# A new order for the first stage of a perceiver layer: context groups, the scaling of x and the weights

## The reference: what is computed

```
x = x + cross_attention(layernorm(x), ctx, w_q, w_k, w_v, w_o)   # 16 heads of 64, 4096 keys
x = x + self_attention(layernorm(x), ...)                        # heads mixed before and after a causal softmax, 16 memory keys
x = x + ffn(layernorm(x), ...)                                   # gated, 16-bit activations, 4-bit weights in blocks of 32

def layernorm(x):  return (x - mean(x)) / sqrt(var(x) + 1e-5)
def cross_attention(query, ctx, ...):
    q, k, v = query @ w_q, ctx @ w_k, ctx @ w_v                  # split into 16 heads
    return concat_heads(softmax(q @ k.T * 64 ** -0.5) @ v) @ w_o
```

## Time and profile before

| | us |
|---|---|
| median of three executions | 1400.45 (1395.76 to 1401.65) |
| the profiled execution | 1400.91 |
| its span on the core | 1398.7 |
| PE busy | 1257.7 (90%) |
| DVE, ACT, POOL busy | 879.3, 723.3, 411.8 |

### The profile page before, as it was taken

One profiled execution on the slowest core, in us unless ns is written; L12 is line 12 of the kernel. 1 busy time (PEld: TensorE's weight loads), 2 busy tenths in 40 slices (PEclk: granted clock), 3 DMA queues, 4 the chain that ended last, 5 costly groups with the idle time before them and its releaser, 6 DMA issues. The chain is left out here.

```text
span 1398.7 us, 21065 instructions
## 1 busy us (share of the span) xinstructions
PE 1257.7 (90%) x8379; PEld 939.1 (67%) x8379; DVE 879.3 (63%) x1042; ACT 723.3 (52%) x1304; POOL 411.8 (29%) x372
## 2 busy tenths in 40 slices
PE   3999999999999999899999999999999697969533
PEld 2786877777786868587868687777778443636312
DVE  5647676766766676547676767676776456513576
ACT  3655556565656556546565655655565231523152
POOL 3605051433425150414342505152342102211010
PEclk9999999999999999999999999999999798979776
DMA  4303020302021133210311203030202354250000
GB/s 154 76 1 74 7 80 1 80 1 80 18 63 50 28 78 93 74 36 2 79 42 39 60 22 79 1 80 1 76 3 63 129 95 55 35 57 1 23 0 15
DMA packets 42528, 68.19 MB, mean 49 GB/s; under 512 B 5040, under 2 KB 31152, under 8 KB 42432
## 3 DMA queue, kind: packets, MB, share of 16 engines
q1 hardware_dynamic: 40896, 66.21, 19.3%
q10 hardware_dynamic: 1536, 0.66, 0.4%
HBM read 25.89 MB, written 0.52 MB: 19 GB/s over the span
## 5 line engine op out<-in xcount | busy, mean ns | idle before, releaser
L455 DVE TENSOR_REDUCE step_max<-score_banks 128x2 f32<-128x1024 f32 x256 | 300.5, 1221 | 122.2 <-PE score_banks L579 122.2
L476 DVE TENSOR_TENSOR prob_sum<-prob_sum,probs 128x1024 f32<-128x1024 f32 x224 | 279.4, 1288 | 139.5 <-ACT probs L406 138.8
L338 POOL TENSOR_TENSOR k_split<-probs,k_split 64x512 fp32r<-64x512 f32 x128 | 163.6, 1278 | 327.6 <-ACT probs L389 323.7
L406 ACT ACTIVATE probs<-score_banks 128x1024 f32<-128x1024 f32 x181 | 181.9, 1028 | 149.4 <-PE out_ps L605 85.3
L593 PE MATMUL score_banks<-q_twice,k_split 128*128 128x256 f32 x724 | 182.2, 288 | 0.2 <-ACT probs L406 0.2
L594 PE MATMUL score_banks<-q_low_max,k_ones 128*128 128x256 f32 x724 | 178.1, 283 | 0.0
L340 POOL TENSOR_TENSOR k_split<-probs,k_split 64x512 fp32r<-64x512 f32 x128 | 163.9, 1281 | 9.6
L593 PEld LDWEIGHTS score_banks<-q_twice,k_split 128*128 128x128 f32 x724 | 138.3, 191 | 11.9 <-issue 6.2
L594 PEld LDWEIGHTS score_banks<-q_low_max,k_ones 128*128 128x128 f32 x724 | 138.5, 191 | 0.0
L331 POOL TENSOR_TENSOR w_lo<-w_raw,w_hi 128x768 fp32r<-128x768 f32 x16 | 36.2, 2260 | 336.5 <-ACT w_hi L357 336.5
L381 ACT ACTIVATE k_split<-key_banks 64x512 fp32r<-64x512 f32 x128 | 75.5, 590 | 104.7 <-PE key_banks L542 104.1
(11 more groups left out here) (207 smaller groups left out, 2169.2 us busy)
## 6 DMA issues: line engine op xcount, KB each, us to landing
k_ones<-k_split SPq DMA_DIRECT2D x128, 256.0 KB, 4.0
ctx_rows<-in_ctx_dram SPq DMA_DIRECT2D x10, 512.0 KB, 3.8
grouped_far<-dots_far SPq DMA_DIRECT2D x32, 136.0 KB
w_raw<-in_L_xattn_w_v_dram SPq DMA_DIRECT2D x14, 256.0 KB, 3.5
probs<-in_ctx_dram SPq DMA_DIRECT2D x6, 512.0 KB, 5.9
w_raw<-in_L_xattn_w_q_dram SPq DMA_DIRECT2D x16, 128.0 KB, 3.5
w_raw<-in_L_xattn_w_k_dram SPq DMA_DIRECT2D x16, 128.0 KB, 3.8
wo_pair<-in_L_xattn_w_o_dram SPq DMA_DIRECT2D x16, 128.0 KB, 2.1
```

The lines of the kernel that those rows point to most:

```text
L338: pool.tensor_tensor(k_split[DH:P, A, keys], keys_staged[j % 2][0:DH], k_split[0:DH, A, keys].bitcast(F32), ALU.subtract).then_inc(k_low[A ...
L406: act.activation(probs[:, j % 2, h, :], scores_of, ACT.Exp, scale=SCALE).then_inc(exp_done, 1)
L455: dve.tensor_reduce(step_max[:, qt, :, j], score_banks[:, 2 * qt:2 * qt + 2, :], X, ALU.max).then_inc(max_done, 1)
L476: dve.tensor_tensor(prob_sum[:, h, :], prob_sum[:, h, :], probs[:, j % 2, h, :], ALU.add).then_inc(sum_done, 1)
```

## The change

The diff reorders the first stage. On DVE, `normalise_rows` gets a callback between the statistics and the scaling, and there the low parts of groups 0, 1 and 2 are made; the copies of `xnT` come behind group 4. On POOL the clearing of the second half of `k_ones` and its row of ones move behind `w_lo` of the first pair. On ACT the row of ones moves into the key loop of the first pair, behind piece 3, and the weights of the first pair are split behind group 2. On SP the weights of the first pair are loaded behind group 0. On PE the first pass transposes groups 0 to 5, with x behind group 4; in the first pair the order is key piece 0, group 6, key piece 1, group 7, and then q. PE, ACT and POOL no longer wait for the constants at the places where they did; SP still does, before it copies into `k_ones`.

```diff
-def normalise_rows(dve, x, out, stats, moments, chain, inverse_std):
+def normalise_rows(dve, x, out, stats, moments, chain, inverse_std, between=None):
...
         dve.bn_aggr(moments[:, t, :], stats[:, t, :]).then_inc(chain, 1)
     n += TOK_TILES
+    if between is not None:
+        between()
     dve.wait_ge(inverse_std, 3)
...
                     sp.dma_start(rows_of(n), ctx_tiles[b, :, tiles, :]).then_inc(ctx_loaded[slot], 16)
-                    if n == SLOTS - 1:
+                    if n == 0:
                         load_weights(0)
...
             pool.wait_ge(inverse_std, 3)
-            pool.memset(k_ones[0:DH, B, :].bitcast(F32), 0.0).then_inc(consts_ready, 1)
-            pool.wait_ge(consts_ready, 4)
-            pool.memset(k_ones[0:1, B, :].bitcast(F32), 1.0).then_inc(consts_ready, 1)
+
+            def zeros_and_ones():
+                pool.memset(k_ones[0:DH, B, :].bitcast(F32), 0.0).then_inc(consts_ready, 1)
+                pool.wait_ge(consts_ready, 4)
+                pool.memset(k_ones[0:1, B, :].bitcast(F32), 1.0).then_inc(consts_ready, 1)
+                pool.wait_ge(consts_ready, 5)
...
                 pool.wait_ge(w_low, it + 1)
+                if it == 0:
+                    zeros_and_ones()
...
-            pool.wait_ge(consts_ready, 5)
             for b in range(BATCH):
                 pairs_of_batch(b, body)
...
-            act.wait_ge(consts_ready, 3)
-            act.activation(k_ones[DH:DH + 1, A, :], ones[DH:DH + 1, 0:1].to_broadcast([1, CTX]), ACT.Copy
-                           ).then_inc(ones_a, 1)
+            def row_of_ones():
+                act.wait_ge(consts_ready, 3)
+                act.activation(k_ones[DH:DH + 1, A, :], ones[DH:DH + 1, 0:1].to_broadcast([1, CTX]), ACT.Copy
+                               ).then_inc(ones_a, 1)
...
                     if j < STEPS and values_behind(i, j) is not None:
                         copy_v(b, i, parity, values_behind(i, j))
+                    if it == 0 and j == 3:
+                        row_of_ones()
...
                         context_high(act, n)
-                        if n == LOADS - 3:
+                        if n == 2:
                             split_weights(0, 0, 0)
-                    act.wait_ge(consts_ready, 5)
...
+            def first_contexts():
+                for n in range(3):
+                    context_low(dve, n)
+
             dve.wait_ge(x_loaded, 16)
-            normalise_rows(dve, x_res, xn, stats, moments, norm_chain, inverse_std)
+            normalise_rows(dve, x_res, xn, stats, moments, norm_chain, inverse_std, first_contexts)
...
-                for n in range(LOADS if b == 0 else 0):
+                for n in range(3, LOADS if b == 0 else 0):
                     context_low(dve, n)
-                    if n == 3:
+                    if n == 4:
                         for c in range(DC):
                             dve.wait_ge(xT_made, c + 1)
...
-                project_q(it, b)
+                if it > 0:
+                    project_q(it, b)
                 pe.wait_ge(w_low, it + 1)
                 wait_past(pe, exp_done, 2 * STEPS * it - 1)
                 for j in range(2):
                     if i == 0:
                         pe.wait_ge(ctx_low, DC * (j + 1 if b == 0 else (b + 1) * LOADS))
                     project_k(it, j)
+                    if it == 0:
+                        transpose_context(6 + j)
+                if it == 0:
+                    project_q(it, b)
...
-                for n in range(LOADS if b == 0 else 0):
+                for n in range(LOADS - 2 if b == 0 else 0):
                     transpose_context(n)
-                    if n == 2:
+                    if n == 4:
                         transpose_x()
                 if b == 0:
                     pe.wait_ge(xT_copied, DC)
-                    pe.wait_ge(consts_ready, 5)
-                    pe.wait_ge(ones_a, 1)
                 pairs_of_batch(b, body)
```

## The result

The changed kernel takes 1406.68 us, the median of six executions (1403.3 to 1407.54), against 1400.45 us for the kernel before. The ratio is 1.0044, with a 95% interval of 1.0029 to 1.0059: it is slower, by 6.2 us. The forecast was 1405.4 us. The profiled execution took 1407.03 us with a span of 1404.8. Its program began 0.52 us later than that of before (POOL's first memset at 9.52 instead of 9.00), so 0.5 us of every later time here is not the change.

A forecast was written before the change was run, and what follows sets the result against it. PE, busy 90% of the span, was taken to bound the kernel, so a later first pair goes through to the end. 4.4 + 0.5 + 0.1 = 5.0 us on 1400.45 gave 1405.4 us, range 1395.5 to 1409.

The forecast's parts named there:

- The meeting: First stage, DVE against POOL: w_lo and two memsets each hold one scaling of x; the scaling ends at 32.3 us.
- S: Start of group 2's high part on ACT, forecast at 20.85 us; the scaling's end was counted from it.
- The chain to the first key piece: From the scaling's end through xnT and PE to ACT's first key copy: 43.85 us against 39.44, 4.4 us later.
- The clock: PE at its lower clock after standing still from about 24 to 32.4 us: 0.5 us taken, up to about 5.
- The loads: First weights loaded behind group 0: PE waits about 1 us before group 1, weights are free 5 us early.
- The row of ones: Moved into pair 0's key loop on ACT: delays ACT's later pieces by at most 3.61 us; 0.1 us taken.
- The faster rival: Scalings pass before POOL, ending at 24.0 us: 3.9 us earlier, 1396.5 us; chance 0.13, including only w_lo holding one.
- The order of start: DVE against POOL: a second scaling just ahead of w_lo still loses (1405.4 us); if it passes, 1401.5 us, chance 0.12.

The follow-up runs named there:

- The two added waits: POOL's wait for all four scalings, before w_lo in the changed kernel (1398.51 us) and before the memsets in the kernel before (1392.96 us).
- the quarters: The changed kernel with the first of the two late memsets cut into four of 1024 columns: 1403.51 us, one execution.
- its repaired form: The kernel before with one wait added, POOL's memsets starting only when the four scalings have ended: 1392.96 us, ratio 0.9954.
- late weights: The changed kernel with the weights loaded behind the first five groups: first profile 1393.46 us, one execution; timed 1400.96 us, median of ten.

## Why the prediction was right, point by point

- *The meeting.* Right as it stood. The four scalings were to meet w_lo, one memset and the other, and end at S + 11.4; they ended at 32.80 with S = 21.55, which is S + 11.25. Counted from the same start, 32.28 against 32.3; S came 0.2 us later than forecast and the meeting was 0.15 shorter. The two added waits show that this collision makes the scaling late, and the quarters show the seam. What the forecast never asked is what the order costs by itself: its 4.4 us are the distance to a kernel whose own collision is nearly as dear. Freed of it on both sides, the new order is 5.6 us behind the old.
- *The chain to the first key piece.* 4.4 us were forecast and 4.9 found, by parts: the scaling's end as forecast, the xnT copies at 35.11 (34.6 counted alike; 34.7 forecast), and 0.5 in the chain from there. In that chain the first key piece ran at the lower clock until 38.6 and took 2.48 us to the group behind it instead of 1.60; the parts behind it were 0.3 shorter than forecast.
- *The clock.* I took 0.5 us, with a bound of 5, for the key pieces and groups behind x alone: the first piece lost 0.9 and the second nothing. The part that was wrong is that I counted the wait of PE for q_twice and the key copies as time, but not as a standstill that lets the clock fall again: 3.62 us without work, then 2.0 us lost at half clock. Keeping PE busy removed exactly that.
- *What I did not forecast*: 1.6 us came back at the change of batch, where the clock had fallen before. The forecast of the median was near (1405.4 for 1406.7) partly by luck, because this and the 2.0 us of the key loop nearly cancel.
- *The loads.* Priced as a wait of 1 us on PE; the wait was 0.96. But I did not see that the weights' place decides the meeting: with them behind group 4, w_lo is late enough in some executions that no memset meets a scaling. My expectation for that run had the same fault.
- *The row of ones.* 0.1 forecast, none found. SP's first copy into `k_ones` came at 58.66 us instead of about 55, and PE did not wait for it.
- *The faster rival* (the scalings get through first, 3.9 us under the kernel before): when POOL waits, the first key piece is 3.6 us earlier than before, so the chain was priced soundly, but the median is only 1.4 us under the kernel before. The price left out the fall of the clock in the key loop, which that run's trace has too, at 38.1 us; it lost 1.0 us there.
- *The order of start.* Here the second scaling started 0.18 us behind w_lo and lost, which the order by the Trainium skill (page "SBUF — State Buffer", section "Who interferes with whom") and rows 4 both give. No run had the second scaling just ahead of w_lo. But other scalings were: the first, 0.14 us ahead of w_lo, took 0.40 us, and with the weights behind group 4 the third, 0.10 us ahead, took 0.41. So a lead of 0.10 us was enough against w_lo, where 0.03 us were not against a memset in rows 4.

## What to carry to other kernels

Before moving work out of the way of another engine, find what else will stand beside it at the new place: here the scaling was moved past two memsets, and the memsets were moved to the same place. Before crediting or blaming a new order, free the old one of the same fault and compare the two: against the kernel before the new order looked 1.4 us better, against its repaired form it was 5.6 us worse. When two engines exclude each other, what counts is the length of the instruction that is met at each seam, so an explicit wait that puts the short ones first (one line, 7 us) is worth more than a new order. A wait that PE has anyway costs more than its length when the clock falls behind it; look at the granted clock of the stretch that follows.

## What the runs showed of the hardware that was not expected

- A scaling (tensor_scalar, fp32, both sides in SBUF) that POOL holds ends about 0.15 us after the POOL instruction (32.80 after 32.65), and exactly one passes in a seam of 0.06 us between two POOL instructions. The hold works both ways: w_lo ended 1.66 to 1.67 us behind the end of the scaling in which it began, whether it had begun 0.24 us ahead of that end (1.92 us long, late weights, timed) or 0.30 (1.96 us, late weights, first profile).
- Which of the two engines goes first can differ between executions of one kernel when no wait ties them; in the two profiles of the kernel with late weights that moved the first key piece by 7.8 us.
- PE's granted clock fell to its lower level during a standstill of 3.62 us, and stayed there until 52.3 us, though PE was busy without a gap from 46.71 us on. The fall can also come when PE is at work again: where POOL waits for the scalings PE began again at 37.51 us, and its clock was 1.00 until 38.1 and 0.50 from 38.2 to 41.5.
